# Which engine's queue issues the joint stage's residual, context and mask loads

## What is computed

```python
x = x + tanh(g_xattn[0]) * L0_xattn(layernorm(x), ctx, ctx, ...)       # strided 16-head attention
x = x + tanh(g_ffn[0])   * L0_ffn(layernorm(x), controller, f1, f2, bias)  # sparse expert layer
x = x + tanh(g_xattn[1]) * L1_xattn(layernorm(x), ctx, ctx, mask)      # softmax(q k^T * D**-0.5 + mask*-1e9) v
x = x + tanh(g_ffn[1])   * L1_ffn(layernorm(x), ln_g, ln_b, w1, w2)    # int8 activations, ternary weights
```

## Time and profile before

| | us |
|---|---|
| median of 3 runs | 1516.33 |
| lowest, highest | 1514.25, 1517.3 |
| the profiled execution | 1514.46 |
| its span, first to last instruction | 1512.7 |
| TensorE, VectorE, ScalarE, GpSimd busy | 1229.6, 988.5, 733.8, 352.1 |
| mean granted clock of TensorE, share of full | 0.89 |

### The profile page before, as it was taken

How to read it: one execution, slowest core, us unless ns; L and a number is a source line. 1 busy time by engine, 2 the same in 40 slices (tenths; PEclk the granted TensorE clock), 3 DMA queues, 4 the chain that set the end, 5 groups by cost and what they waited for, 6 DMA issues and landing times. The chain is left out here.

```text
span 1512.7 us, 24622 instructions
## 1 busy us (share of the span) xinstructions
PE 1229.6 (81%) x8796; PEld 868.7 (57%) x8818; DVE 988.5 (65%) x2309; ACT 733.8 (49%) x1129; POOL 352.1 (23%) x339
## 2 busy tenths in 40 slices
PE   6899999999999845999993999992414998254996
PEld 5788888888888735766651556651313443242442
DVE  5567766667766633444433599994766588776873
ACT  3233333333343321456432466663936555587990
POOL 1233333333343230111000276663000000000010
PEclk9999999999999967999997999995555999556998
DMA  6132222221222119688668999933000677114973
GB/s 207 36 111 73 71 78 85 92 95 70 71 76 91 57 56 363 214 292 309 245 235 325 383 335 332 328 140 138 3 1 2 276 303 305 63 56 159 417 286 141
DMA packets 89717, 261.77 MB, mean 173 GB/s; under 512 B 9584, under 2 KB 21008, under 8 KB 81424
## 3 DMA queue, kind: packets, MB, share of 16 engines
q1 hardware_dynamic: 78976, 226.81, 40.0%
q0 software_dynamic: 7664, 32.51, 6.3%
q10 hardware_dynamic: 2976, 1.14, 0.3%
HBM read 155.32 MB, written 105.12 MB: 172 GB/s over the span
## 5 line engine op out<-in xcount | busy, mean ns | idle before, releaser
L921 PEld LDWEIGHTS p_sel<-p_pick,p_xp 128*128 128x128 bf16 x1536 | 89.2, 100 | 59.2 <-issue 34.1
L921 PE MATMUL p_sel<-p_pick,p_xp 128*128 128x128 bf16 x1536 | 100.5, 223 | 25.5 <-DMA p_xp<-xparts 22.5
L1904 PE MATMUL p_z<-qT,w1T 128*128 128x512 bf16 x501 | 111.2, 382 | 3.0 <-PEq L113 2.5
L1059 DVE COPY p_selT<-p_sel 128x512 f32<-128x512 f32 x64 | 44.3, 692 | 104.3 <-PE p_sel L921 104.3
L2236 POOL DMA_DIRECT2D p_y<-residual x8 | 8.4, 1053 | 401.5 <-POOLq L113 341.6
L2260 PE MATMUL p_o<-w2T,p_Gq 128*128 128x512 bf16 x376 | 86.2, 387 | 6.8 <-DVE p_Gq L2317 6.4
L1963 DVE MAX8 cand<-hid 128x8 f32<-128x128 f32 x384 | 74.7, 276 | 23.9 <-ACT hid L1951 23.9
L1904 PEld LDWEIGHTS p_z<-qT,w1T 128*128 128x128 bf16 x512 | 50.3, 98 | 63.8 <-issue 4.2
L1004 ACT ACTIVATE p_selT<-p_sel 128x512 f32<-128x512 f32 x64 | 38.2, 597 | 91.2 <-PE p_sel L921 91.2
L341 PE MATMUL p_M<-p_ctxTh,p_Wkh 128*128 128x256 f32 x256 | 75.8, 296 | 1.9 <-DVE p_Wkl L667 1.9
L341 PE MATMUL p_M<-p_xnTh,p_Wqh 128*128 128x256 f32 x256 | 75.0, 293 | 1.1 <-DVE p_V L740 1.1
(11 more groups left out here) (319 smaller groups left out, 3499.7 us busy)
## 6 DMA issues: line engine op xcount, KB each, us to landing
inter_d<-p_stage SPq DMA_DIRECT2D x64, 512.0 KB, 4.2
p_rows<-inter_d SPq DMA_DIRECT2D x32, 1024.0 KB, 10.0
activations<-hid SPq DMA_DIRECT2D x24, 1024.0 KB, 3.9
p_cin<-in_ctx_dram SPq DMA_DIRECT2D x32, 512.0 KB, 5.3
xparts<-p_parts SPq DMA_DIRECT2D x16, 768.0 KB, 3.2
hid<-activations SPq DMA_DIRECT2D x10, 1024.0 KB, 9.1
p_xp<-xparts SPq DMA_DIRECT2D x3, 3072.0 KB, 25.2
p_xin<-in_x_dram SPq DMA_DIRECT2D x16, 512.0 KB, 4.2
```

The source lines that it names most:

```text
L921: mm = pe.matmul(bsel[u % 2][:, k * P:(k + 1) * P], xp[:, c, tile, r, :], pick[sb % 2][:, tile, :, :].rearrange("p s g -> p (s g)"), start ...
L1059: dve.tensor_copy(*picked(q, u)).then_inc(s["sel_dve"], 1)
L1904: mm = pe.matmul(bank, w1T[:, c, fc * P:(fc + 1) * P], qT[:, c, bass.ds(first, TB)], start=(c == 0), stop=(c == C - 1))
```

## The change

The loads of the residual, of the context and of the mask, and those of the two gate constants, are taken out of SyncE's stream and issued from ScalarE's. SyncE keeps the identity, the row loads, the layer norm's constants and the stores. On ScalarE the constants come first, then the three loads of sequences 0 and 1, then the wait for the constants; in the loop, the three loads of sequence i+2 come at the end of step i. Before, SyncE issued those of sequence i+1 in its step i. The conditions that each load waits for, buffers and counts are as they were.

```diff
@@ SyncE
-            def load_x(b): ...
-            def load_ctx(b): ...
-            def load_mask(b): ...
             sp.dma_start(ident[:, :], K["c_ident"]).then_inc(s["ident_in"], 16)
             load_rows(0, 0)
             load_rows(0, 1)
-            for dst, src in ((gf_s, gf[0:1]), (gx_s, gx[1:2])):
-                sp.dma_start(dst[:, :], row(src).broadcast_to([P, 1])).then_inc(s["const_in"], 16)
-            load_x(0)
-            load_ctx(0)
             load_rows(1, 0)
-            load_mask(0)
             for i in range(STEPS):
                 if live(i + 1):
                     load_rows(i + 1, 1)
-                    load_x(i + 1)
-                    load_ctx(i + 1)
                 if live(i + 2):
                     load_rows(i + 2, 0)
-                if live(i + 1):
-                    load_mask(i + 1)
...
@@ ScalarE
+            def load_x(b):
+                if b >= XD:
+                    wait_all(act, "hh_done", b - XD + 1)
+                    act.wait_ge(s[f"x_out{b % XD}"], 16 * (b // XD))
+                act.dma_start(xy[b % XD][:, :, :], x_mid[b]).then_inc(s[f"x_in{b % XD}"], 16)
+            def load_ctx(b):
+                if b >= CD:
+                    wait_all(act, "O_full", b - CD + 1)
+                act.dma_start(cin[b % CD][:, :, :], ct[b]).then_inc(s[f"c_in{b % CD}"], 16)
+            def load_mask(b):
+                if b >= 2:
+                    act.wait_ge(s["mask_done"], b - 1)
+                act.dma_start(mk[b % 2]..., mask[b].broadcast_to([P, S])).then_inc(s[f"m_in{b % 2}"], 16)
+            for dst, src in ((gf_s, gf[0:1]), (gx_s, gx[1:2])):
+                act.dma_start(dst[:, :], row(src).broadcast_to([P, 1])).then_inc(s["const_in"], 16)
+            for b in range(2):
+                load_x(b)
+                load_ctx(b)
+                load_mask(b)
             act.wait_ge(s["const_in"], 32)
...
                 if live(i - 2):
                     e_turned(i - 2)
+                if live(i + 2):
+                    load_x(i + 2)
+                    load_ctx(i + 2)
+                    load_mask(i + 2)
```

More of the change, by code:

```diff
@@ L1142, in load_rows @@
                 sp.dma_start(R[b % 2][:, t, :, :], rows[b * NT + t]).then_inc(s[f"r_in{b % 2}{t}"], 16)
[L1144 to L1158, removed]
             def store(b):
@@ L1333, in magnitudes @@
                 act.activation(ha[:, :, :], hid[:, b * NT:(b + 1) * NT, :], ACT.Abs).then_inc(s["abs_done"], 1)
+            def load_x(b):
[10 more added lines that the diff above has]
+                    act.wait_ge(s["mask_done"], b - 1)
+                act.dma_start(mk[b % 2][:, :, :].rearrange("p t k -> p (t k)"), mask[b].broadcast_to([P, S])).then_inc(s[f"m_in{b % 2}"], 16)
+            for dst, src in ((gf_s, gf[0:1]), (gx_s, gx[1:2])):
[4 more added lines that the diff above has]
+                load_mask(b)
             act.wait_ge(s["const_in"], 32)
```

## The result

The changed kernel takes 1603.9 us, the kernel before 1515.55 us in the same session: a ratio of 1.0575, 95% interval 1.0561 to 1.0589. It is 5.75% slower; the forecast was 1598 us.

The account below looks back on a forecast made before the run. TensorE was taken to bound the joint stage's steady part. 1514.5 + 59.2 (serial wait, the start's 2 us gain included) + 25 (clock) = 1598.7; predicted 1598 us, 5.4% slower, range 1566 to 1614.

Parts of the forecast that it names:

- What bounds: Joint stage, steady part: TensorE is the bound, busy 20 of 20 us at 2.4 GHz, 11.57 us a step.
- The waiting engine: End of ScalarE's step: the mask load's wait for scale_mask holds up its later arithmetic and TensorE, +4.9 us a step.
- the sum: Joint stage: forecast terms added up; a full step's cycle of waits comes to 16.44 us in place of 11.57.
- Rival C: ScalarE's spare time takes issues and wait, only the start's gain of 2 to 6 us is left: 1509 to 1513; chance 0.03.
- D: Rival: the change does nothing, TensorE's bound and DMA hide both gain and wait, 1514 us; chance 0.03.
- The clock: TensorE's gaps of 4.74 us: each brings 6.8 us at 1.2 GHz and loses 2.3 us, eleven times, 25 us.
- T0: Joint stage: T0(i) is the time at which TensorE begins the first turn of xn in loop step i.
- the walk: Joint stage, step by step: T0(1) at 838.6, T0(4) at 881.9, T0(14) at 1046.3 against 987.11, +59.2 us.
- Rival A: Joint stage: the serial wait without any clock loss, 1574 us (1566 to 1584); chance 0.24.
- The start: Joint stage's beginning: constants and first loads on ScalarE's queue bring the first mean 2 us sooner, 836.1 instead of 838.24.
- 2 us lost: Worse bound for the joint stage's beginning: ScalarE's transfers take the larger share of the DMA engines.
- the eleventh gap: Last of eleven TensorE idle gaps of 4.74 us in the joint stage, each forecast to lose 2.3 us through the clock.

## Why the prediction was right, point by point

**What bounds.** Right: TensorE bound the steady part, and in the run with the three loads on ScalarE and deeper buffers it still does, at 11.49 us a step.

**The waiting engine.** Right in place and order. The mask issue starts 0.03 us behind scale_mask, ScalarE idles 7.05 us (6 to 7 forecast, counted at full clock), TensorE 4.67 (4.74 forecast), scale_mask takes 0.28 us. With the clock held up the step measured 16.38 us, the sum said 16.44. The residual load goes out first and is hidden, as said: 921.21 against scale_mask's end at 924.74, a margin of 3.5 us where 3.2 was worked out. Rival C, and D, fall with this.

**The clock.** Right that each of these gaps costs clock; place and size were off. The prediction had it fall 2.2 us before T0 and stay down for 6.8 us every time. In stretches of 1 us it is down from about 910.2 to 913.7 around T0 = 910.62, some 3.4 us, and from about 927.3 to 934.1 around T0 = 928.36, some 6.8 us; at 947.44 it fell only behind T0. So the stretches of 20 us above have a clock of 0.83 to 0.91 and not the forecast 0.75 to 0.85. In ten full steps, from T0(4) = 892.66 to T0(14) = 1075.10, a step was 18.24 us, so the clock costs 18.24 - 16.38 = 1.9 us and not 2.3. Seven of the steps are 17.7 to 18.0 long, with a mean clock of 0.88 to 0.90, and three 19.0 to 19.3, with 0.84 or 0.85: the short and the long stretches at 1.2 GHz. But the steps before 4 pay too, which the sum had at full clock: T0(1) to T0(4) was 48.6 us instead of the 43.3 of the walk, at a mean clock of 0.83 to 0.90 (no run holds the clock up there, so that all of the 5.3 us are the clock's is not shown). Rival A, with no cost of the clock, would have been at most 1584 by the run with the matmuls in the gap, which leaves the early steps as they are: the clock's term is at least 20 us of the 88. The walk also had the start too early.

**The start.** Here the step failed. It put the first mean at 17.4 us after the stage's beginning (836.1 against 818.7) by letting two queues share the DMA engines evenly at 378 GB/s. The tanh did come early, 7.0 us into the stage, though not at the 4.3 of the prediction, which counted the issues and not the 6.6 us that the second constant took to land. The first row load landed after 8.4 us (5.8 before), the second tile's scatter began 15.2 us into the stage, and the first mean was at 19.8 us, 0.3 later than before instead of 2.1 sooner. The even share was right: when the second row load landed, near 837.0, sync's queue had moved 2.41 MB and ScalarE's 1.86, together a little over the 4 MB of the prediction. The rate was not: 281 GB/s over the 15.2 us, with 35 GB/s in the first 2.2 us, 78 in the next 2.5 (the slow stretch that goes with the constants' own load, now at the front where the rows need the engines) and 401 only from 829 on. The bound of "2 us lost" covered it, the value taken did not. T0(1) was 2.3 us later than walked.

The sum to T0(14), counted from the stage's beginning and with the clock's 2.3 us for the ten gaps whose cost falls before it, was 250.6 us and came out at 253.2: +2.3 from the start, +5.3 from steps 1 to 3, -5.0 from the ten full steps. That these nearly cancel is luck: the total, 1598 against 1603.9, was closer than the terms deserve. Between the two profiled executions the loss is 90.0 us (1602.7 against 1512.7 of span), where the sum had 84.2: 84.8 up to T0(14), counted from the stage's beginning, 1.9 behind it, where the sum had the eleventh gap's 2.3, and 3.1 ahead of the stage, which vary from run to run; between the medians it is 88.4.

The Trainium skill's rule, "DMA: Bandwidth & Descriptors", section "Issuing engines are not separate DMA queues", was weighed against 2 us of gain at the start. The runs agree with it for the bulk transfers: with the residual, context and mask loads on the second queue and no wait in the way the time was 1518.98 us, not below the kernel before; and the change itself gained nothing at the start.

## What to carry to other kernels

Before a load is moved to another engine's queue, list its waits, and for each ask when it is met in that engine's order, not in the sync queue's. A wait for a buffer that a slower stage frees in the middle of its next step ties the two engines into a circle; here it cost 4.8 us a step and another 1.9 through TensorE's clock, and one step less of lead took all of it back, and two more mask buffers with one more residual buffer all but 0.2%. When one wait is removed, work out which stands behind it: here the store's landing, 2.3 us a step, which the first hid.

## What the runs showed of the hardware

Two loads of one float each, spread over 128 partitions, went with some 2.5 us in which the DMA engines of the core moved 78 to 127 GB/s, at the front of the queues or behind 2 MB of rows; without them that stretch was gone, the first mean of the stage came 2.7 us sooner than with them at the front, and the kernel was 0.24% faster than the kernel before (0.9976, 0.9965 to 0.9987). Whether their size or their number does it, no run isolates. And gaps of 4.67 us on TensorE cost this kernel 20 us more than their own length, through its clock; with 4.46 us of matmuls in them, whose result nobody reads, the clock held at 1.00.
